# Sorted last stage of a four-layer gated transformer block: routing of two chunks in other slots, bias preparation in six pieces

## What is computed

```python
for i in range(4):
    x = x + tanh(g_xattn[i]) * xattn_i(layernorm(x), ctx)     # 16 heads of width 8
    x = x + tanh(g_ffn[i])  * ffn_i(layernorm(x))

# ffn_3, the last part: two of eight experts for each token
h      = x * rsqrt(mean(x * x) + eps) * norm_w
logits = h @ gate_w.T + gate_b
vals, idx = top_k(logits, 2);  wts = softmax(vals)
t1  = einsum('td,efd->tef', h, mlp1_w) + mlp1_b               # 8 experts, 256 columns each
act = swiglu(t1)                  # min(even, 7) * sigmoid(1.702 even) * (clip(odd, -7, 7) + 1)
y   = einsum('tei,edi->ted', act, mlp2_w) + mlp2_b
out = x + sum(y[idx] * wts)
```

## Time and profile before

| what | value |
|---|---|
| time of three runs | 1574.09, 1576.99, 1577.12 us |
| median of the runs | 1576.99 us |
| time of the profiled execution | 1580.99 us |
| its span, first to last instruction | 1579.0 us |
| mean granted TensorE clock in it | 0.867 |
| busy PE, weight loads apart | 1122.7 us (71%), 774.8 us (49%) |
| busy DVE | 1022.0 us (65%) |
| busy POOL | 747.9 us (47%) |
| busy ACT | 709.6 us (45%) |

### The profile page before, as it was taken

How to read it: one execution, slowest core, us unless ns; L and a number is a source line. 1 busy time by engine, 2 the same in 40 slices (tenths; PEclk the granted TensorE clock), 3 DMA queues, 4 the chain that set the end, 5 groups by cost and what they waited for, 6 DMA issues and landing times. The chain is left out here.

```text
span 1579.0 us, 31322 instructions
## 1 busy us (share of the span) xinstructions
PE 1122.7 (71%) x9737; PEld 774.8 (49%) x9737; DVE 1022.0 (65%) x2904; ACT 709.6 (45%) x1435; POOL 747.9 (47%) x816
## 2 busy tenths in 40 slices
PE   3788888238889878978878645312786988788870
PEld 1455555125666656756556422101464656566760
DVE  5577786677666775437677866686566757665452
ACT  1355555114665544445556533211454655444540
POOL 0132430102243345658788767786056424454575
PEclk9999999558999988989999867555898999889895
DMA  8546456035545403322121200230333442123452
GB/s 198 67 75 77 65 68 194 0 50 167 76 58 71 57 28 99 98 61 59 54 55 48 77 4 14 30 110 0 45 50 48 74 61 41 54 75 106 122 155 79
DMA packets 124560, 113.29 MB, mean 72 GB/s; under 512 B 11728, under 2 KB 112720, under 8 KB 123984
## 3 DMA queue, kind: packets, MB, share of 16 engines
q1 hardware_dynamic: 116240, 94.87, 31.5%
q0 software_dynamic: 8192, 16.79, 3.6%
HBM read 44.51 MB, written 29.36 MB: 47 GB/s over the span
## 5 line engine op out<-in xcount | busy, mean ns | idle before, releaser
L1681 DVE TENSOR_REDUCE neg_max<-bank 128x4 f32<-128x512 f32 x384 | 251.5, 684 | 131.9 <-PE bank L1178 130.2
L897 ACT ACTIVATE probs<-bank 128x512 f32<-128x512 f32 x384 | 212.8, 596 | 185.9 <-PE bank L1205 185.0
L1176 PE MATMUL bank<-mask_b,ident_b 128*128 128x512 bf16 x384 | 154.9, 403 | 83.3 <-DMA k_rows<-area 39.2
L1178 PE MATMUL bank<-k_rows,q_rows 96*128 96x256 bf16 x768 | 155.0, 284 | 0.0
L890 ACT ACTIVATE q_rows<-bank 32x512 bf16<-32x512 bf16 x192 | 102.9, 582 | 115.7 <-PE bank L1188 112.1
L694 POOL CAST area<-area 128x1024 bf16<-128x1024 f32 x36 | 37.3, 1036 | 224.2 <-DMA k_rows<-area 173.9
L1195 PE MATMUL bank<-ident_b,mask_b 128*128 128x512 bf16 x384 | 136.2, 396 | 3.0 <-ACT probs L897 1.8
L1205 PE MATMUL bank<-q_rows,k_rows 128*128 128x128 bf16 x1536 | 138.1, 224 | 0.0
L613 POOL TENSOR_SCALAR rstd_a<-meanvar 128x4 f32<-128x4 f32 x30 | 6.9, 230 | 274.4 <-DVE meanvar L1637 195.0
L1205 PEld LDWEIGHTS bank<-q_rows,k_rows 128*128 128x128 bf16 x1536 | 114.3, 101 | 29.0 <-issue 4.7
L1219 PE MATMUL bank<-probs,v_aug 128*32 128x128 f32 x3072 | 111.7, 287 | 0.6
(11 more groups left out here) (257 smaller groups left out, 2841.9 us busy)
## 6 DMA issues: line engine op xcount, KB each, us to landing
q_rows<-area SPq DMA_DIRECT2D x144, 128.0 KB
k_rows<-area SPq DMA_DIRECT2D x288, 64.0 KB
ctxT<-ctx_t SPq DMA_DIRECT2D x24, 256.0 KB, 8.8
moe_rows<-m2b SPq DMA_DIRECT2D x4, 1536.0 KB, 15.2
q_rows<-moe_rows SPq DMA_DIRECT2D x24, 256.0 KB
moe_rows<-work SPq DMA_DIRECT2D x24, 256.0 KB
room<-moe_rows SPq DMA_DIRECT2D x24, 256.0 KB
moe_rows<-v_aug SPq DMA_DIRECT2D x24, 256.0 KB
```

Of the source, the lines that this page charges most:

```text
L897: act.activation(probs[j].rearrange("p a b -> p (a b)"), T_BANK[j % 2][:], ACT.Exp).then_inc(exp_done, 1)
L1176: pe.matmul(dst[:], ident_b[:], bcast(mask(b, t), 4), start=True, stop=False)
L1178: mm = pe.matmul(dst[:, 256 * i:256 * i + 256], q_rows[b][SCORE_ROWS, 2 * j + i, tok], k_rows[b][SCORE_ROWS, :, 2 * j + i, tok], start=Fal ...
L1681: dve.tensor_reduce(neg_max[:, 4 * j:4 * j + 4], S_BANK[j % 2][:].rearrange("p (h k) -> p h k", h=4), AX.X, ALU.max, negate=True).then_inc ...
```

## The change

**Biases.** `split_biases` no longer has two parts in groups 0 and 1 but six pieces of 512 columns (`GT`), each with the same five steps over its columns, and piece 0 the scaling of the down weights besides. They stand at the end of POOL's loop body, behind `add_bias`, in groups 0 to 5. The semaphore `bias3_ready` counts six pieces; SP and TensorE wait for six ahead of the last stage. POOL's loop is written out for this attention, so that each group can name its piece.

**Last stage.** On DVE the statistics of chunk 3 go from slot 4 to slot 3, the normalisations from slots 2 and 6 to 1 and 5, `choose` from 5 and 9 to 3 and 7, `put` from 7 and 11 to 5 and 9. On TensorE `turn_routed` goes from slots 4 and 8 to 2 and 6, `ranks` from 6 and 10 to 4 and 8. The adds of groups 0, 1, 2 in slots 18, 20, 22 become adds of groups 0 to 4 in slots 12, 16, 18, 20, 22. On POOL the scatter of chunk 1 is cut in two halves with `route_std` of chunk 3 between, and the gathers of group 0 stand between the scatters of chunks 2 and 3.

```diff
@@ -386,10 +386,10 @@
         XSTART = ((1, 2), (NG + 1, NG + 2), (2 * NG + 6, 2 * NG + 7))
         START = ((0, 1), (16, 17), (29, 30))
         EARLY = 5
-        TURN3 = {4: 4, 8: 6}
-        RANK3 = {6: 2, 10: 3}
+        TURN3 = {2: 4, 6: 6}
+        RANK3 = {4: 2, 8: 3}
         SCALE3 = 4
-        TAKEN3 = {18: 0, 20: 1, 22: 2}
+        TAKEN3 = {12: 0, 16: 1, 18: 2, 20: 3, 22: 4}
 
         FFN2_STATS = {16: 0, 17: 1, 18: 2, 19: 3, 20: 4, 24: 5, 28: 6}
         FFN2_NORM = {17: 0, 18: 1, 19: 2, 20: 3, 21: 4, 25: 5, 29: 6}
@@ -561,7 +561,7 @@
                     store(k)
 
             def sorted_rows3():
-                sp.wait_ge(bias3_ready, 1)
+                sp.wait_ge(bias3_ready, NG - 2)
 
                 def load(k):
                     if k % NQ == 0:
@@ -634,21 +634,20 @@
                 pool.wait_ge(pool_steps, ch.count)
                 pool.tensor_tensor(r_stds, r_stds_a, minus_half[:], ALU.pow).then_inc(r_rstd_ready, 1)
 
-            def split_biases(part):
-                if part == 0:
+            def split_biases(piece):
+
+                if piece == 0:
                     pool.wait_ge(experts_loaded, 16 * 5)
-                    counted(pool.tensor_copy(bias3, raw3))
-                    counted(pool.tensor_tensor(raw3, raw3, bias3, ALU.subtract))
-                    return
-                pool.wait_ge(split_ready, G0[2] + 4)
-                waits_apart(pool)
-                at = slice(P // 2, P)
-                counted(pool.tensor_copy(bias3[at], raw3[at]))
-                counted(pool.tensor_tensor(raw3[at], raw3[at], bias3[at], ALU.subtract))
-                at = slice(3 * P // 4, P)
-                counted(pool.tensor_copy(bias3[at], raw3[at]))
-                down3 = w_e3.rearrange("p (e w) -> p e w", e=E)[:, :, 2 * P:]
-                pool.tensor_scalar(down3, down3, 1.0 / 1.702, None, ALU.mult).then_inc(bias3_ready, 1)
+                    down3 = w_e3.rearrange("p (e w) -> p e w", e=E)[:, :, 2 * P:]
+                    counted(pool.tensor_scalar(down3, down3, 1.0 / 1.702, None, ALU.mult))
+                at = slice(GT * piece, GT * (piece + 1))
+                counted(pool.tensor_copy(bias3[:, at], raw3[:, at]))
+                counted(pool.tensor_tensor(raw3[:, at], raw3[:, at], bias3[:, at], ALU.subtract))
+                mid, low = slice(P // 2, P), slice(3 * P // 4, P)
+                counted(pool.tensor_copy(bias3[mid, at], raw3[mid, at]))
+                counted(pool.tensor_tensor(raw3[mid, at], raw3[mid, at], bias3[mid, at], ALU.subtract))
+                pool.tensor_copy(bias3[low, at], raw3[low, at]).then_inc(bias3_ready, 1)
+                pool.wait_ge(bias3_ready, piece + 1)
 
             def counted(ins):
                 ins.then_inc(pool_steps, ch.one())
@@ -730,10 +729,6 @@
                         if left >= 2:
                             inv_std(L0[a] + gr + 3)
                             split(gr + 2, a)
-                        if a == 2 and is_first:
-                            split_biases(0)
-                        if a == 2 and first and b == 1:
-                            split_biases(1)
                         if left == 1:
                             route_std(NCH * (a - 1))
                         if left == 0:
@@ -743,8 +738,14 @@
                                 add_bias(TG * (gr - 1) + t)
                         if left == 1:
                             route_std(NCH * (a - 1) + 1)
+                        if a == 2 and left >= 2:
+                            split_biases(gr)
                 pool.wait_ge(setup_dve, 2)
-                walk(pool, body, ch, 10)
+                if a == 1:
+                    walk(pool, body, ch, 10)
+                else:
+                    for gp in range(0, NG, 2):
+                        body(gp, gp == 0, gp == NG - 2)
                 for t in range(TG):
                     add_bias(NT - TG + t)
 
@@ -763,11 +764,13 @@
 
             def feed_forward3():
                 route_std(NCH + 2)
-                scatter(NCH + 1)
+                scatter(NCH + 1, range(TG))
                 route_std(NCH + 3)
+                scatter(NCH + 1, range(TG, TC))
                 scatter(NCH + 2)
+                gather3(0)
                 scatter(NCH + 3)
-                for g in range(NG):
+                for g in range(1, NG):
                     gather3(g)
 
             def feed_forward0():
@@ -1504,7 +1507,7 @@
                 pe.wait_ge(heads_read, 3 * NT)
                 pe.wait_ge(maxT_ready, 6 * NT)
                 pe.wait_ge(r_read, R0[2] + 3 * NT)
-                pe.wait_ge(bias3_ready, 1)
+                pe.wait_ge(bias3_ready, NG - 2)
                 weights_at = {}
 
                 def turn_blk(k):
@@ -2174,17 +2177,17 @@
                     clip(2 * k)
                     if k:
                         hide(2 * k - 1)
-                    if k in (0, 4):
-                        route_stats(NCH + 2 + k // 4)
-                    if k - 2 in (0, 4):
-                        route_norm(NG + 4 + 2 * ((k - 2) // 4))
-                        route_norm(NG + 5 + 2 * ((k - 2) // 4))
-                    if k in (5, 9):
-                        choose(NCH + 2 + (k - 5) // 4)
+                    if k in (0, 3):
+                        route_stats(NCH + 2 + k // 3)
+                    if k in (1, 5):
+                        route_norm(NG + 4 + 2 * (k // 5))
+                        route_norm(NG + 5 + 2 * (k // 5))
+                    if k in (3, 7):
+                        choose(NCH + 2 + (k - 3) // 4)
                     clip(2 * k + 1)
                     hide(2 * k)
-                    if k in (7, 11):
-                        put(NCH + 2 + (k - 7) // 4)
+                    if k in (5, 9):
+                        put(NCH + 2 + (k - 5) // 4)
                     if k in TAKEN3:
                         add_taken3(TAKEN3[k])
                 hide(2 * NK - 1)
```

## The result

Four runs of the changed kernel took 1554.16 to 1566.71 us, median **1564.22**; four of the kernel before (the three known ahead and one of 1586.85) had the median 1577.05. The ratio over all these runs is 0.990 with a 95% interval of 0.9859 to 0.9942; that of the two medians is 0.992. So the kernel became faster, by 12.8 us between the medians; 1561.5 was predicted, in a range of 1551 to 1570. The profiled execution took 1563.16 us (span 1561.2), against 1580.99 (1579.0).

A forecast was written before the change was run, and what follows sets the result against it. POOL's instruction queue was taken to set the end. Gains of 4.5 us in the third attention and 11.0 in the last stage, together 15.5, off the median 1576.99 gave 1561.5, range 1551 to 1570.

The forecast's parts named there:

- spacings, sum: Third attention: the five distances between POOL's split ends total 147.2 us, 9.0 less than 156.2.
- piece 5 on route_std for chunk 0: End of third attention: the last bias piece stands before POOL's route_std for chunk 0, charged 4.5 us (0 to 5.5).
- add in slot 16: Last stage, DVE: the moved add starts at 1495.9, its gathers landing at 1494.6 to 1495.9, just in time.
- The cover: Third attention: the spread DMA's 21.1 us after a split hides a piece, k being read at 20.9; nothing left over.
- The new wait: Last stage: half of chunk 1's scatters wait behind route_std for chunk 3, turning block 6 7.4 us later.
- first hole in POOL's queue: Last stage before the change: POOL's gap from 1411 to 1435.0, read as a wait for DVE's put.
- Pieces fully covered: Rival, third attention: spacing as in the second attention, 15.3 + 11.0 us gained, 1550.7; chance 0.13.
- Gathers unbroken: Rival, last stage: the last store is early, 4.5 + 16.2 us gained, 1556.3; chance 0.13.
- Statistics a slot late: Rival, last stage: everything behind block 6 moves by 5.3 us, 1566.8; chance 0.11.
- nothing comes sooner: Rival, last stage: statistics 11 us later than placed, 1572.5, near no change; chance 0.06.
- Lock on top of the wait: Rival, third attention: DVE also blocked 1.2 us in each of six groups, 7.2 in all, 1568.7; chance 0.06.
- pieces fully exposed: Rival, third attention: each piece lengthens the loop by its full 4.6 us; 1581.1, slower; chance 0.06.

The follow-up runs named there:

- e1: Kernel before with the six bias pieces alone, last stage as before; 1572.36 us against 1577.70, ratio 0.9982.
- e9: Kernel before with the six bias pieces between inv_std and split, last stage as before; 1562.39 us against 1577.31, ratio 0.9882.
- e7: Kernel before with only the gathers of group 0 put between the scatters of chunks 2 and 3; 1570.70 us against 1579.86, ratio 0.9931.
- e6: Changed kernel with group 0's gathers behind chunk 3's scatter and adds in slots 18, 20, 22; 1563.68 us against 1579.86 for the kernel before, ratio 0.9902.
- e4: Changed kernel with each bias piece between a group's inv_std and its split; 1550.27 us against 1577.70 for the kernel before, ratio 0.9843.
- e3: Changed kernel with chunk 1's 16 scatters in one run, chunk 3's route_std behind; 1555.07 us against 1577.70 for the kernel before, ratio 0.9862.
- e5: Changed kernel with the edits of e3 and e4 together; 1541.50 us against 1579.86 for the kernel before, ratio 0.9762.

## Why the prediction was right, point by point

The first scatter of chunk 1 started at 1391.18 before and at 1383.73 after, so 7.45 us are added to the times of the stage after, to set them beside the forecast.

| step | forecast | measured |
|---|---|---|
| spacings, sum | 147.2 | 147.7 |
| first spacing, mean of the other four | 30.4, 29.2 | 31.7, 29.0 |
| one piece | 4.6 | 4.4 |
| piece 5 on route_std for chunk 0 | 4.5 | 7.30 - 2.88 = 4.4 |
| **attention, net** | **4.5** | **4.0** |
| route_std for chunk 3 may start | 1404.9 | 1405.1 |
| second half of chunk 1's scatter | 1408.8 | 1408.8 |
| block 6 turned | 1422.8 | 1423.2 |
| scatter of chunk 2 | 1432.3 | 1432.6 |
| gathers of group 0 | 1452.9 | 1453.3 |
| scatter of chunk 3 | 1463.0 | 1463.6 |
| the other 56 gathers | 1483.3 | 1484.1 |
| add in slot 16 starts | 1495.9 | 1495.4 |
| last store landed | 1538.5 | 1538.8 |
| gathers of group 6, POOL's wait | 1538.8, 4.8 | 1539.5, 4.35 |
| last gather | 1557.7 | 1558.3 |
| **stage** | **11.0** | **10.4** |

*The steps held.* The piece's wait was covered as worked out from one group: the norm waits 1.95 to 2.83 us for rstd behind the first spacing (2.9 forecast), and the spacing stays near 29. The cover was used up, as forecast: three of those four splits are now released by ACT's copy of the projection, 20.8 and 20.9 us after the split before in two of them and 22.2 in the third, and one by the spread DMA. The new wait came where it was placed and cost block 6 what it was said to cost. TensorE's loop came out later, not sooner, and made the hole before the gathers of group 6. The add in slot 16 was just in time: it waited 0.51 us for its gathers, in DVE's timeline:

```profile
1487.97 2.34 DVE L2144 SCALAR_TENSOR_TENSOR x<-k_rows,m2b,x 128x128 f32<-128x128 f32 x8 [0.51 <-DMA k_rows<-moe_rows,m2b]
```

Part of the close sum is luck: the first spacing came out 1.3 longer than forecast and the other four together 0.7 shorter. The sum, 15.5, was 1.1 too large, and the stretch between attention and stage lost 0.8 that no edit explains: it took 75.9 to 80.1 us in the profiled executions of before, after and e1 to e9, which all have the same work there. The rest of the 2.7 us between 1561.5 and 1564.22 is inside the spread of the runs, 12.6 us. Two of the signs were drawn too tight: the longest of DVE's 128x16 casts lasts 1.52 us, against "under 1.5", and the mean of all five spacings is 29.55, against "29.5 or more" as a sign of being wrong. And of the first hole in POOL's queue that the prediction names, 1411 to 1435.0, only 20.20 us are the wait for `put`; route_std for chunk 3 stands ahead of it.

*What the sum didn't see.* It made the stage's gain out of a chain, from the sooner slots through chunk 3's sooner scatter to the gathers. It had the true bound of the changed kernel, the last store and 16 gathers, but didn't say that a single line would come within 3 us of it. e7 shows that the gather between the scatters alone does, and e6 that the sooner slots alone do too, both by POOL's queue and not by the store. The size was right; the work of the two edits was not told apart.

*The rivals.* "Pieces fully covered" fell by the first spacing (31.7) and the tail (4.4); e4 shows that it was to be had, by another place. "Gathers unbroken" fell by the hole of 4.35; in e6 and e7 the gathers do run unbroken to the end, but because POOL comes to group 6 later and not because the store is early. "Statistics a slot late" and "nothing comes sooner" fell: chunk 3's statistics came within 0.2 us of the forecast. "Lock on top of the wait" and "pieces fully exposed" fell by spacings of 28.6 to 30.0 behind the first.

*Two rules beside the rows.* DVE's 1.12 us beside a subtract of 1.15 and the norm of 2.29 in e4 (the subtract's end at 1178.83 and the norm's own 1.11 give 1179.9, and it ended at 1180.1) agree with the Trainium skill, "SBUF — State Buffer", section "Who interferes with whom". As the prediction held, that hold costs little where DVE has to wait in any case, and in e4 hardly more; but the prediction's bound for it, one subtract or 1.2 us, is too low for the norm's 1.3 to 1.7 us in the other groups of e4. The other rule, in "DMA: Bandwidth & Descriptors" of the Trainium skill, stands in the section "Issuing engines are not separate DMA queues" and not in the one that the prediction names; it says of DMAs in general that the sequencer's time to start one is usually small beside it. By it, as the prediction reads it, the stage's gain would have been nothing. The row decided rightly: the last 16 gathers still start (1550.82 - 1532.09)/15 = 1.249 us apart with no other release, and the stage gained 10.4.

## What to carry to other kernels

When an engine's instruction stream sets the end, look first for its waits and for work behind them that is already allowed: here eight gathers moved into a hole gave, in one line, about what a whole reweaving of slots gave, and the two didn't add, because another bound, the last store, lay 2.8 us behind. Before cutting a run of transfers to let a small step through, price what stands behind the cut, since the second half inherits the step's wait. And put filler work behind the small result that others wait for and ahead of the engine's own long wait, not between the two.

## What the runs showed of the hardware

In e4 a DVE norm of four tiles took 2.29 us instead of 1.11 while POOL ran a subtract of 1.16 us, so the loss there is about one POOL instruction long; over the six groups it was 1.2 to 1.7 us, and nearly all of it was absorbed. The indirect DMAs kept their pace in every order tried: in the median 1.25 us from gather to gather and 1.26 or 1.27 from scatter to scatter, whether they stood in runs of 4, 8, 16 or 64. And at the same wait for a table, 3.02 and 3.07 us long, TensorE's granted clock stayed at 1.00 (2.4 GHz) in e3 and fell to 0.73 on average, toward the lower level of 1.2 GHz, in e5, two kernels with one program in the last stage; with the fall the next block took 1.7 us longer.
